# First graph layer: destination sums as three more columns of the crossing product, weights loaded inside the layer

## The reference

```python
# layer 0
gathered = edge_val[:, None] * x[edge_col]                       # edge_col = dst
support  = segment_sum(gathered, edge_row, num_segments=6250)    # edge_row = src
out      = relu(concatenate([x, support], axis=1) @ W + b)
x        = layernorm(x + out)
# later layers need, for each destination node:
#   segment_sum(edge_weight, dst)      (layer 2, the bias's share)
#   segment_sum(gate, dst) + 1         (layer 3, the degree)
#   how many edges end there           (layer 1, where its edges begin and end)
```

## Time and profile before

| | before |
|---|---|
| time, median of 3 runs | 7195.86 us (7192.72 to 7196.65) |
| the profiled execution's own time | 7208.19 us |
| its span in the trace | 7203.6 us |
| busy, share of the span | PE 82%, PEld 56%, DVE 50%, ACT 20%, POOL 70% |
| mean granted TensorE clock | 0.884 |
| DMA | 1521.26 MB, mean 211 GB/s |
| scatter stage, first to last scatter | 114.81 to 1698.02 us |

### The profile page before, as it was taken

How to read it: one execution, slowest core, us unless ns; L and a number is a source line. 1 busy time by engine, 2 the same in 40 slices (tenths; PEclk the granted TensorE clock), 3 DMA queues, 4 the chain that set the end, 5 groups by cost and what they waited for, 6 DMA issues and landing times. The chain is left out here.

```text
span 7203.6 us, 114186 instructions
## 1 busy us (share of the span) xinstructions
PE 5941.4 (82%) x29640; PEld 4051.3 (56%) x29640; DVE 3635.0 (50%) x13335; ACT 1463.3 (20%) x4664; POOL 5068.3 (70%) x4600
## 2 busy tenths in 40 slices
PE   3888888886737888876777779997999899989997
PEld 2555555555624555544454556665666566656665
DVE  4444544443535666656777734444344333444555
ACT  2333333332211222212344311111000000010000
POOL 3777777777756777757767757664777677767776
PEclk9788878887868999987777779998999999999998
DMA  8999998985324444436655569885999799979996
GB/s 289 214 189 189 192 186 186 189 188 114 100 81 111 116 117 116 117 98 190 189 179 184 161 221 296 282 282 182 308 308 312 236 310 307 307 243 314 306 314 226
DMA packets 784760, 1521.26 MB, mean 211 GB/s; under 512 B 157736, under 2 KB 485340, under 8 KB 781828
## 3 DMA queue, kind: packets, MB, share of 16 engines
q1 hardware_dynamic: 499828, 974.55, 40.2%
q0 software_dynamic: 282256, 515.62, 31.4%
q10 hardware_dynamic: 2304, 26.74, 0.9%
HBM read 1220.44 MB, written 295.98 MB: 211 GB/s over the span
## 5 line engine op out<-in xcount | busy, mean ns | idle before, releaser
L751 POOL DMA_INDIRECT rows<-gcn_rows,source x1632 | 1626.5, 997 | 599.5 <-issue 463.7
L829 PEld LDWEIGHTS bank<-onehots,rows 128*128 128x128 f32 x8704 | 1157.2, 194 | 635.5 <-issue 502.8
L1993 POOL DMA_INDIRECT support<-rows,index x784 | 1218.1, 1554 | 381.7 <-DMA support<-rows,index 199.4
L829 PE MATMUL bank<-onehots,rows 128*128 128x128 f32 x8704 | 1209.3, 280 | 192.9 <-DMA rows<-gcn_rows,source 111.1
L1279 POOL DMA_INDIRECT rows<-gat_rows,index x784 | 741.5, 946 | 295.0 <-issue 210.7
L1578 POOL DMA_INDIRECT rows<-gat_rows,source x544 | 663.1, 1219 | 304.2 <-issue 156.2
L751 POOL DMA_INDIRECT rows<-norm,source x544 | 517.2, 951 | 290.1 <-issue 150.8
L2132 PE MATMUL rows_bank<-x_window,cross 128*128 128x256 f32 x1568 | 654.8, 510 | 78.9 <-ACT cross L2110 78.2
L1368 PE MATMUL bank<-onehots,rows 128*128 128x128 f32 x3136 | 551.4, 299 | 134.0 <-DVE rows L1424 133.3
L877 DVE TENSOR_SCALAR onehots<-iota,half_offset,edge_values 128x128 f32<-128x128 f32 x2176 | 605.9, 359 | 26.4 <-issue 7.0
L844 PE MATMUL dense_bank<-stripped,edge_space 128*128 128x512 f32 x1176 | 569.1, 607 | 13.6 <-issue 13.6
(11 more groups left out here) (371 smaller groups left out, 8922.0 us busy)
## 6 DMA issues: line engine op xcount, KB each, us to landing
alpha<-matrix SPq DMA_DIRECT2D x483, 512.0 KB
matrix<-matrix SPq DMA_DIRECT2D x448, 512.0 KB
matrix<-zeros SPq DMA_DIRECT2D x196, 512.0 KB
edge_space<-gcn_rows SPq DMA_DIRECT2D x588, 128.0 KB
source_row<-in_src_flat SPq DMA_DIRECT2D x198, 256.0 KB, 5.1
dst_row<-in_dst_flat SPq DMA_DIRECT2D x68, 512.0 KB
support<-zeros ACTq DMA_DIRECT2D x16, 1632.0 KB, 28.4
rows<-gcn_rows,source POOLq DMA_INDIRECT x1632
```

Source lines behind the costliest of these rows:

```text
L751: nc.gpsimd.indirect_dma_start(rows[:, k, :], None, table, bass.IndirectOffsetOnAxis(ap=g.source[:, at:at + 1], axis=0),).then_inc(gathere ...
L829: done = nc.tensor.matmul(by_chunk(banks[h])[:, c, :], rows[:, k, c * P:(c + 1) * P], onehots[:, k, :], start=first and c == 0, stop=final ...
L1993: nc.gpsimd.indirect_dma_start(support[k % COPIES], bass.IndirectOffsetOnAxis(ap=index[:, k // HALF, k % HALF:k % HALF + 1], axis=0), rows ...
```

## The change

Three things are changed.

1. The three destination sums become columns 128 to 130 of the crossing product: `same_source` gets three more columns with the edge's values (a copy on VectorE for each tile), the matmul makes 131 columns, and ACT, after `cross`, copies the three columns (one row for each destination of the window) to `half_counts`. The counts matmul and the copy of `values` go. `add_counts` on VectorE, at the sixth tile of the next half, adds the half's eight tiles; `turn_sums` on TensorE, before the fifth tile's crossing, turns the sums by a product with the identity; `add_histogram` at the end of that half adds them to `histogram`. So a half's sums arrive half a ring later than before.
2. `load_weights` goes. Its nine DMAs are appended to `later`, one in each of nine more written-out rings, and the fold is the last work of VectorE in `degrees`.
3. POOL writes the spare rows before it waits for `support_zeroed`, not after.

```diff
-        same_source = sbuf("same_source", [P, BUFS, P])
+        same_source = sbuf("same_source", [P, BUFS, P + 3])
+        half_counts = sbuf("half_counts", [P, 2, HALF, 3])
+        half_sum = sbuf("half_sum", [P, 2, 3])
...
-                if first_pass:
-                    pool.wait_ge(g.support_zeroed, 16 * 2 * HALF)
                 for slot in range(HALF):
                     for part in range(2):
                         pool.dma_start(spare[slot, part], zeros[:, 0:P]).then_inc(scattered[slot], 16)
                 for slot in range(HALF):
                     pool.wait_ge(scattered[slot], 32)
+                if first_pass:
+                    pool.wait_ge(g.support_zeroed, 16 * 2 * HALF)
...
+                    later += g.weight_loads
...
                         if k % HALF == 0:
-                            nc.scalar.copy(values[:, k // HALF, :, :],
-                                           g.edge_values[:, bass.ds(i * RING + k, HALF), :]
-                                           ).then_inc(s.values_ready, 1)
+                            act.wait_ge(s.summed, i * 2 + (k // HALF + 2))
                         act.wait_ge(s.crossed, i * RING + (BUFS + k + 1))
-                        nc.scalar.copy(cross[:, k % BUFS, :], cross_bank[k % 2][:, 0:P]).then_inc(s.cross_copied, 1)
+                        nc.scalar.copy(cross[:, k % BUFS, :], cross_bank[k % 2][:, 0:P])
+                        nc.scalar.copy(half_counts[:, k // HALF, k % HALF, :], cross_bank[k % 2][:, P:P + 3]
+                                       ).then_inc(s.cross_copied, 1)
...
+                def turn_sums(i, h):
+                    pe.wait_ge(s.summed, i * 2 + (h + 3))
+                    pe.wait_ge(s.counted, i * 2 + (h + 1))
+                    nc.tensor.matmul(counts_bank[h][0:3, 0:P], half_sum[:, 1 - h, :], g.identity[:],
+                                     start=True, stop=True).then_inc(s.turned, 1)
...
+                        if k % HALF == HALF // 2:
+                            turn_sums(i, k // HALF)
...
-                        nc.tensor.matmul(cross_bank[k % 2][:, 0:P], onehots[:, b, :], same_source[:, b, :],
-                                         start=True, stop=True)
-                        if k % HALF == 0:
-                            pe.wait_ge(s.values_ready, i * 2 + (k // HALF + 1))
-                            pe.wait_ge(s.counted, i * 2 + (k // HALF + 1))
-                        nc.tensor.matmul(counts_bank[k // HALF][0:3, 0:P], values[:, k // HALF, k % HALF, :],
-                                         onehots[:, b, :], start=(k % HALF == 0), stop=(k % HALF == HALF - 1)
-                                         ).then_inc(s.crossed, 1)
+                        nc.tensor.matmul(cross_bank[k % 2][:, 0:P + 3], onehots[:, b, :], same_source[:, b, :],
+                                         start=True, stop=True).then_inc(s.crossed, 1)
...
+                def add_counts(i, h):
+                    dve.wait_ge(s.cross_copied, i * RING + (HALF * h + 2))
+                    nc.vector.tensor_reduce(half_sum[:, 1 - h, :], half_counts[:, 1 - h, :, :].rearrange("p k v -> p v k"),
+                                            AXX, ALU.add).then_inc(s.summed, 1)
...
+                            nc.vector.tensor_copy(same_source[:, b, P:P + 3],
+                                                  g.edge_values[:, tile, :].rearrange("p a v -> p (a v)"))
...
+                            if k == HALF // 2 + 1:
+                                add_counts(i, h)
...
-                        dve.wait_ge(s.crossed, i * RING + (BUFS + HALF * (h + 1)))
-                        dve.wait_ge(s.counted, i * 2 + (h + 2))
-                        nc.vector.tensor_tensor(histogram[:, window], histogram[:, window],
-                                                counts_bank[h][0:3, 0:P], ALU.add).then_inc(s.counted, 1)
+                        add_histogram(i, h)
...
                 inverse_root(nc, link, degree, g.root_degree, scratch)
+                fold(link)
```

More of the change, by code:

```diff
@@ L2168, in _ @@
                     multiply(i, RING - 1)
+                turn_sums(g.tiles // RING, 0)
             @block.vector
@@ L2240, in _ @@
                         index_half(i, 1 - h, h)
[L2241 to L2246 removed]
+                        add_histogram(i, h)
+                add_counts(g.tiles // RING, 0)
+                add_histogram(g.tiles // RING, 0)
 def write_matrix(nc, g, pool, first, count):
@@ L2530, in _, with degrees @@
                             ALU.mult, ALU.add).then_inc(s.added, 1)
-def degrees(nc, g, histogram, beside):
+def degrees(nc, g, histogram, beside, fold):
     with ExitStack() as stack:
@@ L3558, in on_all @@
     return bias.unsqueeze(0).to_broadcast([P, bias.shape[0]])
-def load_weights(nc, pairs, factors):
-    with ExitStack() as stack:
-        sbuf, _ = tiles_of(stack, nc)
-        widest = max(weight.shape[1] for _, weight, _, _ in factors)
-        att = sbuf("att", [P, len(factors), 2, widest])
-        each = sbuf("each", [P, 2, 2, widest])
-        with phase(nc, "own", "loaded") as (block, s):
-            @block.sync
-            def _(sync):
-                for f, (factor, weight, att_src, att_dst) in enumerate(factors):
-                    n = weight.shape[1]
-                    sync.dma_start(factor[:, :, 0:n], by_rows(weight)).then_inc(s.loaded, 16)
-                    for k, a in enumerate((att_src, att_dst)):
-                        sync.dma_start(att[:, f, k, 0:n], a.rearrange("h c -> (h c)").unsqueeze(0).to_broadcast([P, n])
-                                       ).then_inc(s.loaded, 16)
-                for tile, dram in pairs:
-                    sync.dma_start(tile, dram).then_inc(s.loaded, 16)
-                sync.wait_ge(s.loaded, 16 * (3 * len(factors) + len(pairs)))
-            @block.vector
-            def _(dve):
-                link = linker(dve, s.own)
-                dve.wait_ge(s.loaded, 16 * (3 * len(factors) + len(pairs)))
-                for f, (factor, weight, att_src, att_dst) in enumerate(factors):
-                    heads, n = att_src.shape[0], weight.shape[1]
-                    for c in range(2):
-                        for k in range(2):
-                            done = nc.vector.tensor_tensor(each[:, c, k, 0:n], factor[:, c, 0:n], att[:, f, k, 0:n],
-                                                           ALU.mult)
-                    link(done)
-                    for c in range(2):
-                        for k in range(2):
-                            done = nc.vector.tensor_reduce(factor[:, c, n + k * heads:n + (k + 1) * heads],
-                                                           each[:, c, k, 0:n].rearrange("p (h v) -> p h v", h=heads),
-                                                           AXX, ALU.add)
-                    link(done)
@@ new lines, in weight_loads, with fold_attention @@
+def weight_loads(pairs, factors, att):
+    loads = []
+    for f, (factor, weight, att_src, att_dst) in enumerate(factors):
+        n = weight.shape[1]
+        loads.append((factor[:, :, 0:n], by_rows(weight)))
+        for k, a in enumerate((att_src, att_dst)):
+            loads.append((att[:, f, k, 0:n], a.rearrange("h c -> (h c)").unsqueeze(0).to_broadcast([P, n])))
+    return loads + list(pairs)
+def fold_attention(nc, link, factors, att, each):
+    for f, (factor, weight, att_src, att_dst) in enumerate(factors):
+        heads, n = att_src.shape[0], weight.shape[1]
+        for c in range(2):
+            for k in range(2):
+                done = nc.vector.tensor_tensor(each[:, c, k, 0:n], factor[:, c, 0:n], att[:, f, k, 0:n], ALU.mult)
+        link(done)
+        for c in range(2):
+            for k in range(2):
+                done = nc.vector.tensor_reduce(factor[:, c, n + k * heads:n + (k + 1) * heads],
+                                               each[:, c, k, 0:n].rearrange("p (h v) -> p h v", h=heads),
+                                               AXX, ALU.add)
+        link(done)
@@ L3701, in build_program @@
                 set_up(nc, g, t, support, zeros[:])
-                load_weights(nc, ((top[:], by_rows(t.L0_gnn_W[0:features, :])),
-                                  (bottom[:], by_rows(t.L0_gnn_W[features:, :])), (bias[:], on_all(t.L0_gnn_b))),
-                             ((factor1, t.L1_gnn_W1, t.L1_gnn_att_src1, t.L1_gnn_att_dst1),
-                              (factor2, t.L1_gnn_W2, t.L1_gnn_att_src2, t.L1_gnn_att_dst2)))
+                factors = ((factor1, t.L1_gnn_W1, t.L1_gnn_att_src1, t.L1_gnn_att_dst1),
+                           (factor2, t.L1_gnn_W2, t.L1_gnn_att_src2, t.L1_gnn_att_dst2))
+                att = tiles_of(first, nc)[0]("att", [P, len(factors), 2, features])
+                each = tiles_of(first, nc)[0]("each", [P, 2, 2, features])
+                g.weight_loads = weight_loads(((top[:], by_rows(t.L0_gnn_W[0:features, :])),
```

(5 more changed lines are left out.)

18 lines of the change are left out of this document (12 added, 6 removed).

## The result

| | after |
|---|---|
| time, median of 20 runs beside 20 of before | 7214.19 us, before 7195.81 us |
| ratio, 95% interval | 1.0022, 1.0016 to 1.0028: slower by 16 us |
| span of the profiled execution | 7200.7 us |
| mean granted TensorE clock | 0.856 |
| scatter stage, first to last scatter | 90.50 to 1694.02 us |

The profiled execution after is one of the quicker of its kind (its own time is 7202.82 us, 11.4 under the median) and that of before one of the slower (7208.19, 12.4 over its median), so the two spans must not be subtracted. In these two executions the scatter stage took 1583.2 us before and takes 1603.5 now; from the last scatter to the end it is about 5506 us in both. So here the change gives 24.3 us at the stage's start and loses 20.3 in the stage.

A forecast was written before the change was run, and what follows sets the result against it. POOL's scatters and their landings, slowed by DMA traffic, were taken to bound the scatter stage. Start -13 and bursts +24 give +11 us, on the median of 7195.86 a forecast of 7207 us (+0.15%), its own range 7191 to 7221.

The forecast's parts named there:

- three near-equal cases: Whole kernel against the 0.2% bound: faster 0.25, within 0.39, slower 0.36.
- The start: Scatter stage's start: first scatter at 92.4 us instead of 114.8, -22.4; in all -13 us (-20 to -3).
- +6.6 for bytes moved beside scatters: Early scatter stage: 3.3 MB more of SP's loads go beside scatters, at 2.0 us a megabyte, +6.6 us.
- +2.6 for the weights: Scatter stage: 1.3 MB of weights loaded in nine more written-out rings beside scatters, +2.6 us.
- The matmul, the histogram and the copies at 0: Scatter stage: TensorE, ACT and VectorE work stands behind a 9 us lead over POOL, price 0.
- The fold: End of degrees: the moved fold, under 5.6 us, lies under 13.7 us of cover by POOL's writes, price 0.
- The bursts, +24: SP's loads at the ring's end go out tight: 0.5 us a ring over 48 rings, +24 us (0 to +54).
- 0.63: Ring's end in the kernel before: the loose burst of loads costs POOL about 0.63 us a ring.
- 1 (the bursts don't matter): SP's bursts in the scatter stage don't matter, or even pace softens them: 7183 us (7172 to 7192); chance 0.27.
- 2 (the end burst becomes as dear as the middle one): Ring's end burst costs 1.13 us a ring: +54 - 13 = +41, 7237 us; chance 0.20.
- 3 (TensorE becomes the bound through its clock): Scatter stage: with less work TensorE's clock stays slow, +194 us at worst, 7390; chance 0.03.
- 4 (the counts mattered): Scatter stage: POOL's 74.7 us of waits were TensorE's doing and go, 117 us less, 7066; chance 0.05.

The follow-up runs named there:

- experiment 1: Changed kernel with the weight loads, the fold and the spare writes back where they were before, so the sums alone; 7218.8 us, ratio 1.0027.
- experiment 2: Kernel before with only the weight loads, the fold and the spare writes moved, old sums kept; 7190.6 us, ratio 0.9988.
- 9: Changed kernel with each half's second zeroing behind its second quarter, and the first half's quarters waiting 2 and 1 tiles more; 7152.5 us, ratio 0.9937.
- 6: Kernel before with the weight loads part alone, and each half's second zeroing behind its second quarter of source rows; 7154.4 us, ratio 0.9930.
- experiment 11: Changed kernel with each half's second zeroing behind its second quarter, and the quarters waiting 3, 2, 3 and 2 tiles more; 7135.2 us, ratio 0.9914.
- 7: Changed kernel with SP's two quarters of source rows in the ring's first half waiting for 4 and 3 tiles more; 7170.7 us, ratio 0.9957.
- experiment 12: Kernel before with SP's x window of the ring's second half waiting for one product more; 7241.0 us, ratio 1.0055.
- 5: Kernel before with each half's second zeroing moved in SP's queue behind the half's second quarter of source rows; 7156.2 us, ratio 0.9940.
- experiment 10: Kernel before with weight loads inside, second zeroings behind the second quarters, and the quarters waiting 2, 1, 2 and 1 tiles more; 7185.6 us, ratio 0.9984.
- experiment 8: Changed kernel with second zeroings behind the second quarters, and the tail's keys load released before VectorE's wait for the spare block; 7172.8 us, ratio 0.9955.
- 4: Changed kernel with each half's second zeroing moved in SP's queue from behind the x window to behind the second quarter; 7156.2 us, ratio 0.9948.

## Why the prediction was nearly right

The forecast was 7207 us and "no change that can be measured" as the likeliest of three near-equal cases; it is 7214, in the forecast's own range, and just past the 0.2% bound.

**The start.** The spare writes landed by 82.97 us (81.5 predicted) and the first scatter went at 90.50 (92.4): the writes came 1.5 us later, and the way from them to the scatter took 7.5 us, not 10.9, so two small errors partly cancel. That the three queues take turns one for one holds; packets between 66 and 70 us after (q10 ACT's zeroing, q1 SP, q0 POOL):
```profile
q10 hardware_dynamic: 83, 0.95, 59.8%
q1 hardware_dynamic: 89, 0.35, 23.1%
q0 software_dynamic: 91, 0.19, 14.5%
```
Not foreseen was VectorE's wait for `tail_row`: SP's queue was costed as bytes, and no step asked which of its loads the second tile needs. It takes 3.9 us off the gain. Of the other terms, +6.6 for bytes moved beside scatters was too large: from 1 to after, the first 320 scatters take 3.4 us longer in all, no more than the late second one. And +2.6 for the weights was too small: the 144 scatters of the nine rings beside which they ride take 4.5 us longer from 1 to after, 4.7 from before to 2. One more transfer in the ring-end group raises its waits in these rings from 0.36 us (before) to 0.95 (2), which the term, a price by bytes, left out. With the first scatter 20.4 and 21.3 us earlier in these pairs of traces, the sum is -12.5 and -13.3, as forecast. By the times the part is worth -9 (-16 to -1) in experiment 2, and -4 from 1 to after; within what was allowed, and smaller.

**The matmul, the histogram and the copies at 0.** Right in substance. ACT's 3-column copies take 175 ns and VectorE's 201, more than the 170 assumed by little, and end 10.6 us before POOL. At like spacing (9 against 6) the new sums stand 5 us above the old, less than the intervals can tell, and the 24 us are not theirs. VectorE's wait before the histogram, which was to vanish, is 76.1 us, 67.5 of it without a releaser. The fold ran from 1732.32 to 1736.54 us, and POOL's writes went on to 1746.7, so it was covered as forecast.

**The bursts, +24.** The mechanism and its size were right, and this is the step that carried the forecast: the sums part measured +19 and +24. The ring-end group's waits rose by 0.55 us a ring (0.51 in the last 20 rings), 0.5 predicted. That it fell so close is partly luck: 0.5 was picked between 0 and 1.13 and not worked out, and half or double of it would have had the same reasons. Wrong was a detail that decides nothing here: the group was to go out within 1.7 us and takes 2.1 on average to its second zeroing. The 1.76 us that two waits behind one tight group had given was a fair measure too: the mid-ring group averages 1.88 before.

**What was underrated** is how much of the kernel's time hangs on the same mechanism. The argument priced only the step from 0.63 to somewhat more. Both groups together were 2.67 us a ring before, 131 us of the kernel, and experiment 11 brings that to 1.38.

**The rivals.** 1 (the bursts don't matter) falls by experiments 7 and 12. 2 (the end burst becomes as dear as the middle one) was the direction but not the size: 1.34 against 1.72; experiment 12 gets near it, with 1.52 against 1.84, when the group is tightened further, at +39 us, and the rival's price was +54 for its burst. 3 (TensorE becomes the bound through its clock) falls, though the clock did go down. In the middle stretch it is 0.68, from 0.82, a mix with more of the 1.2 GHz level in it, after TensorE's work there fell. The Trainium skill's rule ("TensorE: Matmul & The Clock Gate", The HAM clock gate), slow unless activity lifts it, agrees with that; the busy share alone doesn't give the mean clock, though, which was 0.75 with TensorE busy 58% of the last stretch before. The bound asked for a mean under 0.56, and TensorE is idle 22% of the stretch. (The prediction's own figures, 939 us of work falling to 741, are a fifth less work, not the third that it names.) 4 (the counts mattered) falls by experiment 1: without them POOL issues no faster.

What stays open: an own cost of the sums of a few microseconds, 17 at the most that the intervals allow; and why after some groups one wait is released by ACT's copy of rows (1.33 us at 937.96) and after others by the landing alone. ACT waits there for a landing itself, which frees its slot, so I count both as the same wait; no run took them apart.

## What to carry to other kernels

Where one queue's indirect accumulating DMAs set the pace and another queue's loads run beside them, look at when the loads go out, not only at how many bytes they are: experiments 12 and 5, both the kernel before with an edit to this queue alone, move the same bytes and differ by 85 us. By the ring's waits some 46 of these are the ring-end group's, whose five transfers go out within 3.4 us in one and 8.3 in the other, and some 40 the mid-ring group's, which 5 spreads as well. A change that frees an engine moves the semaphores that pace the load queue, and so can pull loads together that a stall had kept apart; list for each load what it waits for, and whether that wait will still be the last. Pace such a queue on purpose, with waits in it spread over the ring, and check the gap to the next group as well: experiment 10 lost 31 to 39 us to a delay that ran into it. An occasional extra load in a group that is already there isn't free either: nine weight loads cost 4.5 to 4.7 us here, an estimate by bytes alone said 2.6.

## What was not expected of the hardware

Waits behind a group of transfers come late: in the rows above two idle times of 0.85 to 1.33 us (0.30 of each is spacing), 8 to 12 us after the x window; over all rings of the changed kernel nine tenths of the ring-end waits lie 7 to 14 us behind it. A likely reason is in the program: a scatter may be issued once the fourth before it has landed, four times 1.85 us, so a group that holds up one landing would show up that much later on POOL and nowhere near the transfers that caused it. The traces give no landing times of the scatters, so this is not shown. And the price falls unevenly with spacing: a first quarter moved from 1.4 to 2.2 us behind the x window was worth 0.15 us a ring, less than one trace can tell, one moved to 5.5 (with the last transfer from 5.3 to 10.6) 0.96.

A load issued 17 to 18 us earlier into queues that were full (experiment 8) released VectorE at 93.5 us, and the same load without the edit at 92.6 to 92.7 (after, 4).
